# The last mixing of a four-block graph network: the weighed sum made on TensorE instead of VectorE

## The reference, cut to what matters

```
topk_vals, topk_idx = jax.lax.top_k(gate_logits, K)          # K = 2 of 16 experts
topk_w = jax.nn.softmax(topk_vals, axis=-1)
...
moe = jnp.sum(topk_w[..., None] * sel, axis=2)               # the two experts' outputs, weighed
y = x + moe
mu = jnp.mean(y, axis=-1, keepdims=True)
var = jnp.var(y, axis=-1, keepdims=True)
return (y - mu) / jnp.sqrt(var + EPS) * gamma + beta
...
x = x + _L1_ffn_ref(_layernorm(x, axis=-1)[None], ...)[0]
```

## Time and profile before

| what | value |
| --- | --- |
| median of 3 runs | 1766.2 us (1765.77 to 1766.2) |
| the profiled execution | 1768.76 us |
| its span (first to last instruction) | 1766.9 us |
| mean granted TensorE clock | 0.899 of full |
| PE busy | 1476.3 us (84%) |
| DVE busy | 869.2 us (49%) |
| ACT busy | 476.8 us (27%) |
| POOL busy | 337.7 us (19%) |

### The profile page before, as it was taken

One profiled execution on the slowest core, in us unless ns is written; L12 is line 12 of the kernel. 1 busy time (PEld: TensorE's weight loads), 2 busy tenths in 40 slices (PEclk: granted clock), 3 DMA queues, 4 the chain that ended last, 5 costly groups with the idle time before them and its releaser, 6 DMA issues. The chain is left out here.

```text
span 1766.9 us, 34489 instructions
## 1 busy us (share of the span) xinstructions
PE 1476.3 (84%) x8498; PEld 1032.0 (58%) x8499; DVE 869.2 (49%) x2496; ACT 476.8 (27%) x1228; POOL 337.7 (19%) x391
## 2 busy tenths in 40 slices
PE   4795999989998999957999947998997759999920
PEld 3674754457444845536998923445664648898810
DVE  6896743233232467773222257213887542222258
ACT  2464410012000311112444423001222314444421
POOL 3000210012000300013445510000000514545420
PEclk9955999999999999977999979998999569999965
DMA  4000321123111422221323267202221434333344
GB/s 122 0 0 11 99 84 47 50 84 119 48 47 54 128 90 86 84 95 65 113 92 126 80 184 217 71 24 81 72 71 30 156 125 128 121 100 97 124 129 128
DMA packets 134622, 158.41 MB, mean 90 GB/s; under 512 B 16929, under 2 KB 119698, under 8 KB 134258
## 3 DMA queue, kind: packets, MB, share of 16 engines
q1 hardware_dynamic: 122642, 125.59, 22.5%
q0 software_dynamic: 11840, 32.12, 6.1%
q10 hardware_dynamic: 96, 0.20, 0.0%
HBM read 103.12 MB, written 57.93 MB: 91 GB/s over the span
## 5 line engine op out<-in xcount | busy, mean ns | idle before, releaser
L885 PE MATMUL layer_ps<-parts,counts 128*128 128x512 f16 x1875 | 413.4, 382 | 1.3 <-issue 0.6
L885 PEld LDWEIGHTS layer_ps<-parts,counts 128*128 (+1 forms) x1875 | 184.5, 98 | 221.3 <-issue 8.7
L1526 ACT ACTIVATE experts_hT<-experts_ps_h,experts_b_col 128x128 f32<-128x128 f32 x456 | 166.2, 368 | 223.7 <-PE experts_ps_h L1501 142.4
L1509 PE MATMUL experts_ps_y<-experts_rows,experts_hT 128*128 128x256 f32 x688 | 165.0, 381 | 1.3 <-ACT experts_hT L1526 0.9
L1464 POOL DMA_INDIRECT chosen<-experts_y,experts_row x116 | 114.9, 991 | 140.2 <-issue 127.1
L1453 POOL DMA_INDIRECT experts_fetched<-tokens,experts_index x120 | 116.4, 970 | 105.6 <-issue 66.3
L1550 DVE COPY experts_xT<-experts_ps_x 128x256 f32<-128x256 f32 x114 | 48.4, 425 | 174.3 <-PE experts_ps_x L1490 157.6
L1509 PEld LDWEIGHTS experts_ps_y<-experts_rows,experts_hT 128*128 128x128 f32 x688 | 123.5, 191 | 17.4 <-ACT experts_hT L1526 3.7
L786 POOL TENSOR_TENSOR parts<-layer_rest,gru_rows 128x256 f32 (+2 forms) x75 | 54.6, 728 | 406.9 <-DVE layer_rest L761 406.9
L1501 PE MATMUL experts_ps_h<-experts_xT,experts_rows 128*128 128x128 f32 x976 | 122.1, 279 | 11.3 <-issue 10.2
L1501 PEld LDWEIGHTS experts_ps_h<-experts_xT,experts_rows 128*128 128x128 f32 x976 | 118.9, 194 | 19.9 <-issue 16.2
(11 more groups left out here) (310 smaller groups left out, 2072.8 us busy)
## 6 DMA issues: line engine op xcount, KB each, us to landing
experts_rows<-in_L_ffn_w SPq DMA_DIRECT2D x32, 512.0 KB
gru_rows<-x SPq DMA_DIRECT2D x75, 128.0 KB, 2.1
own<-layer_own SPq DMA_DIRECT2D x75, 128.0 KB, 1.7
layer_own_in<-own SPq DMA_DIRECT2D x75, 128.0 KB, 2.1
h<-layer_out SPq DMA_DIRECT2D x50, 128.0 KB, 1.7
gru_rows<-h SPq DMA_DIRECT2D x50, 128.0 KB, 2.1
gru_rows<-chosen SPq DMA_DIRECT2D x50, 128.0 KB, 2.4
combine_y<-chosen SPq DMA_DIRECT2D x50, 128.0 KB, 2.1
```

Source lines behind the costliest of these rows:

```text
L885: last = nc.tensor.matmul(ps[b][:], cst.counts[:, s, bass.ds(t * P, P)], parts[:, s, :], start=s == 0, stop=s == NT - 1)
L1509: last = nc.tensor.matmul(ps_y[:, 0:D], hT[:, c, :], down[b][:, c, :], start=c == 0, stop=c == KH - 1)
L1526: nc.scalar.activation(hT[:, c, :], ps_h[c][:, 0:P], function, bias=b1_col[:, bass.ds(e * KH + c, 1)]).then_inc(hT_ready, 1)
```

## The change

TensorE now makes the weighed sum. ScalarE writes, for each tile, two 128x128 matrices that hold a tile's weights on the diagonal (the identity times a weight a row). TensorE multiplies them with y0 and y1 and the identity with `tokens`, and sums all three in one of four product banks (PSUM). VectorE reads the statistics and the centring from the bank. SyncE's store of a tile is issued one step later, behind the load that follows.

```diff
-        mixed, out, small = pair("mixed", [P, D]), pair("out", [P, D]), pair("small", [P, 10])
-        normal, scale, w_loaded = pair("normal", [P, D]), sb("gamma", [P, D]), sem("w_loaded")
+        weigh = [pair(f"weigh{c}_", [P, P]) for c in range(2)]
+        out, small, normal = pair("out", [P, D]), pair("small", [P, 10]), pair("normal", [P, D])
+        scale, w_loaded = sb("gamma", [P, D]), sem("w_loaded")
+        ps = [ctx.enter_context(nc.psum_tensor(tag + f"ps{b}", [P, BANK], F32)) for b in range(B)]
...
-        loop = lambda engine, step: tile_loop(engine, step, n=B, ahead=2, behind=2)
+        loop = lambda engine, step: tile_loop(engine, step, n=B, ahead=2, behind=B)
...
                 def step(k, b):
                     t = k * B + b
-                    sp.wait_ge(taken, t + 1)
+                    sp.wait_ge(mixed, t + 1)
                     if not past(t + B):
                         load(t + B, b)
-                    sp.wait_ge(ready, t + 1)
-                    if past(t + 1):
...
+                    if not early(t - 1):
+                        store(t - 1, b - 1)
...
+            @block.tensor
+            def _(pe):
+                def step(k, b):
+                    t = k * B + b
+                    pe.wait_ge(got[b], k * 32 + 32)
+                    pe.wait_ge(weights_ready, t + 1)
+                    if not early(t - B):
+                        pe.wait_ge(centred, t - (B - 1))
+                    for c in range(2):
+                        nc.tensor.matmul(ps[b][:, 0:D], weigh[c][b % 2][:], y[b][c][:], start=c == 0, stop=False)
+                    nc.tensor.matmul(ps[b][:, 0:D], cst.ident[:], tile_of(tokens, t), start=False, stop=True).then_inc(mixed, 1)
+
+                loop(pe, step)
 
             @block.scalar
             def _(act):
                 nc.scalar.preload_act_table(ACT.Sqrt)
 
+                def spread_weights(t, b):
+                    if not early(t - 2):
+                        act.wait_ge(mixed, t - 1)
+                    nc.scalar.activation(weigh[0][b][:], cst.ident[:], ACT.Copy, scale=plan.weight[0][:, bass.ds(t, 1)])
+                    nc.scalar.activation(weigh[1][b][:], cst.ident[:], ACT.Copy,
+                                         scale=plan.weight[1][:, bass.ds(t, 1)]).then_inc(weights_ready, 1)
+
                 def step(k, b):
-                    act.wait_ge(var_ready, k * B + b + 1)
+                    t = k * B + b
+                    if not past(t + 2):
+                        spread_weights(t + 2, b % 2)
+                    act.wait_ge(var_ready, t + 1)
                     norm_root(nc, cst, small[b % 2]).then_inc(std_ready, 1)
 
+                for t in range(2):
+                    spread_weights(t, t)
                 loop(act, step)
...
                 def norm_of(u, b):
-                    nc.vector.scalar_tensor_tensor(normal[b][:], mixed[b][:], small[b][:, 6:7], scale[:], ALU.subtract,
+                    nc.vector.scalar_tensor_tensor(normal[b % 2][:], ps[b][:, 0:D], small[b % 2][:, 6:7], scale[:], ALU.subtract,
                                                    ALU.mult).then_inc(centred, 1)
...
-                    dve.wait_ge(got[b], k * 32 + 32)
-                    nc.vector.scalar_tensor_tensor(mixed[d][:], y[b][0][:], plan.weight[0][:, bass.ds(t, 1)],
-                                                   tile_of(tokens, t), ALU.mult, ALU.add).then_inc(begun, 1)
+                    dve.wait_ge(mixed, t + 1)
+                    nc.vector.bn_stats(small[d][:, 0:6], ps[b][:, 0:D])
                     if behind:
                         if early(t - 2):
                             dve.wait_ge(w_loaded, 16)
                         inverse_of(t - 1, before_d)
-                        norm_of(t - 1, before_d)
-                    dve.wait_ge(begun, t + 1)
-                    nc.vector.scalar_tensor_tensor(mixed[d][:], y[b][1][:], plan.weight[1][:, bass.ds(t, 1)], mixed[d][:],
-                                                   ALU.mult, ALU.add).then_inc(taken, 1)
+                        norm_of(t - 1, (b - 1) % B)
+                    dve.drain()
+                    nc.vector.bn_aggr(small[d][:, 6:8], small[d][:, 0:6]).then_inc(var_ready, 1)
                     if behind:
-                        dve.wait_ge(inverted, t)
-                        dve.wait_ge(centred, t)
                         last_of(t - 1, before_use, before_d)
-                    dve.wait_ge(taken, t + 1)
-                    nc.vector.bn_stats(small[d][:, 0:6], mixed[d][:])
-                    dve.drain()
-                    nc.vector.bn_aggr(small[d][:, 6:8], small[d][:, 0:6]).then_inc(var_ready, 1)
...
                 inverse_of(u, d)
-                dve.drain()
-                norm_of(u, d)
-                dve.drain()
+                norm_of(u, (NT - 1) % B)
                 last_of(u, use, d)
```

More of the change, by code:

```diff
@@ L1803, in combine @@
         y = [[sb(f"y{b}_{c}", [P, D]) for c in range(2)] for b in range(B)]
-        mixed, out, small = pair("mixed", [P, D]), pair("out", [P, D]), pair("small", [P, 10])
-        normal, scale, w_loaded = pair("normal", [P, D]), sb("gamma", [P, D]), sem("w_loaded")
+        weigh = [pair(f"weigh{c}_", [P, P]) for c in range(2)]
+        out, small, normal = pair("out", [P, D]), pair("small", [P, 10]), pair("normal", [P, D])
+        scale, w_loaded = sb("gamma", [P, D]), sem("w_loaded")
+        ps = [ctx.enter_context(nc.psum_tensor(tag + f"ps{b}", [P, BANK], F32)) for b in range(B)]
         got = [sem(f"got{b}") for b in range(B)]
         stored = [sem(f"stored{b}") for b in range(2)]
-        var_ready, std_ready, taken = sem("var_ready"), sem("std_ready"), sem("taken")
-        begun, inverted, centred, ready = sem("begun"), sem("inverted"), sem("centred"), sem("ready")
-        loop = lambda engine, step: tile_loop(engine, step, n=B, ahead=2, behind=2)
+        weights_ready, mixed, var_ready, std_ready = sem("weights_ready"), sem("mixed"), sem("var_ready"), sem("std_ready")
+        inverted, centred, ready = sem("inverted"), sem("centred"), sem("ready")
+        loop = lambda engine, step: tile_loop(engine, step, n=B, ahead=2, behind=B)
         buffer = lambda k, b: (k * 2 + b // 2, b % 2)
@@ L1822, in step, with store @@
                     t = k * B + b
-                    sp.wait_ge(taken, t + 1)
+                    sp.wait_ge(mixed, t + 1)
                     if not past(t + B):
                         load(t + B, b)
-                    sp.wait_ge(ready, t + 1)
-                    if past(t + 1):
-                        sp.dma_start(output[t * P:N_NODES, :], out[b % 2][0:LAST, :]).then_inc(stored[b % 2], 16)
+                    if not early(t - 1):
+                        store(t - 1, b - 1)
+                def store(u, b):
+                    sp.wait_ge(ready, u + 1)
+                    if past(u + 1):
+                        sp.dma_start(output[u * P:N_NODES, :], out[b % 2][0:LAST, :]).then_inc(stored[b % 2], 16)
                     else:
-                        sp.dma_start(output[rows(t), :], out[b % 2][:]).then_inc(stored[b % 2], 16)
+                        sp.dma_start(output[rows(u), :], out[b % 2][:]).then_inc(stored[b % 2], 16)
                 for b in range(B):
@@ L1836, in _ @@
                 tile_loop(sp, step, n=B, ahead=B, behind=2)
+                store(NT - 1, NT - 1)
                 for b in range(2):
                     sp.wait_ge(stored[b], 16 * uses(b))
+            @block.tensor
[10 more added lines that the diff above has]
+                loop(pe, step)
             @block.scalar
@@ L1851, in _, with inverse_of, last_of @@
             def _(dve):
+                def inverse_of(u, d):
+                    dve.wait_ge(std_ready, u + 1)
+                    nc.vector.reciprocal(small[d][:, 9:10], small[d][:, 8:9]).then_inc(inverted, 1)
                 def norm_of(u, b):
-                    nc.vector.scalar_tensor_tensor(normal[b][:], mixed[b][:], small[b][:, 6:7], scale[:], ALU.subtract,
+                    nc.vector.scalar_tensor_tensor(normal[b % 2][:], ps[b][:, 0:D], small[b % 2][:, 6:7], scale[:], ALU.subtract,
                                                    ALU.mult).then_inc(centred, 1)
[L1856 to L1860, removed]
+                def last_of(u, use, d):
+                    dve.wait_ge(centred, u + 1)
+                    dve.wait_ge(inverted, u + 1)
                     if not early(u - 2):
-                        dve.wait_ge(stored[b], use * 16)
-                    nc.vector.scalar_tensor_tensor(out[b][:], normal[b][:], small[b][:, 9:10], tile_of(base, u), ALU.mult,
+                        dve.wait_ge(stored[d], use * 16)
+                    nc.vector.scalar_tensor_tensor(out[d][:], normal[d][:], small[d][:, 9:10], tile_of(base, u), ALU.mult,
                                                    ALU.add).then_inc(ready, 1)
@@ L1870, in step @@
                     t = k * B + b
-                    use, d = buffer(k, b)
```

(19 more changed lines are left out.)

## The result

The changed kernel took 1751.81 us (median of 4 runs, 1750.59 to 1754.42) against 1765.99 us for the kernel before (median of 4, 1763.86 to 1766.2): 14.2 us less, a ratio of 0.9925 with a 95% interval of 0.9913 to 0.9937. Measured beside it two more times, on two different chips, the ratio was 0.9915 (0.9898 to 0.9931) and 0.9923 (0.9903 to 0.9943). The forecast was 1752.7 us, 13.5 less than a median of 1766.2.

What follows compares the result with a forecast made beforehand. VectorE's operations, a plain sum, bound the last stage; the start, loop tiles at 1.78 us, written-out tiles at 1.58 and the tail end it at 1748.2 against 1761.7, 13.5 less: 1752.7 us, 8-in-10 range 1748 to 1760.

Steps and rivals of the forecast that it cites:

- Two operations off VectorE's sum: Last stage: the two weighing operations leave VectorE (0.79 to 0.80 us a tile); its remaining five steps sum to 1.68.
- The loop's edge: Loop of the last stage, once in four tiles: taken as 2.353 - 2.32 us a tile, bringing VectorE's step to 1.71.
- A bank as source: VectorE reading a product bank instead of SBUF: extra cost put at 0, bounds -0.05 to +0.06 us a read.
- The loop's tile of 1.78: Forecast time per loop tile in us, from VectorE's 1.71 and SyncE's about 1.75 with hitches; bounds 1.60 and 2.0.
- SyncE's queue: Loop of the last stage: SyncE's three DMAs a tile were to take about 1.75 us, level with VectorE's 1.71.
- third rival: Loop step of 2.1 us instead of 1.78, by register work behind the drain or by transfers: 5.1 us more, 1757.8; chance 0.10.
- ScalarE's copies: Two 128x128 weight copies a tile on ScalarE: at most 0.84 us, some 1.4 with root and register work, hidden below 1.78.
- The start: Head of the last stage: bank 0 done 2.77 us after 1700.7, bank 1 at 1706.05, TensorE's clock rising after 5 us.
- The last four tiles: Written-out tiles at the stage's end, waits being constants: 1.58 us each, statistics of tile 20 at 1739.35, tile 24 at 1745.65.
- The tail behind the last statistics: End of VectorE's work: 0.93 us to the aggregation, 0.55 to the reciprocal, then 0.07, 0.52 and 0.48.
- TensorE as the bound: Rival: TensorE stays at 1.2 GHz, 2.56 us a tile in the last stage, 5.8 us slower, 1772; chance 0.07.

Runs made afterwards that it cites:

- four_one: Changed kernel with four output buffers instead of two and one 256 KB load a tile instead of two of 128: 1744.19 us, ratio 0.9903 to the kernel before.
- order_only: Kernel before with only the new order of operations and the later store, VectorE still making the weighed sum: 1766.92 us against 1765.55 before.
- one_load: Changed kernel with one 256 KB load a tile in place of two of 128 KB, same bytes: 1748.72 us, ratio 0.9918 to the kernel before.
- one_y: Changed kernel with the second expert's load left out, 256 KB of traffic a tile instead of 384: 1744.40 us, ratio 0.9902 to the kernel before.
- warm: Changed kernel with five extra 128x128 identity matmuls on TensorE at the head of the stage: 1748.56 us, ratio 0.9920 to the kernel before.

## Why the prediction was right

- **Two operations off VectorE's sum.** Right. The steps I gave as 0.34, 0.07, 0.52, 0.35 and 0.40 are 0.34, 0.07, 0.55, 0.32 and 0.40 in the tile above; both sums are 1.68. Over a whole round of four tiles it is less: in four_one, where VectorE waits for no store, aggregation to last operation is 0.23, 0.34, 0.31 and 0.23, and the tile 1.65. With the order alone (order_only) nothing is gained.
- **The loop's edge.** Misread. I spread 0.03 us a tile over ten tiles, but only one edge lies in them:

```profile
1738.14 0.42 DVE L1890 BATCH_NORM_STATS2 combine_small<-combine_mixed 128x6 f32<-128x256 f32 x1
...
1739.18 0.48 DVE L1875 SCALAR_TENSOR_TENSOR combine_mixed<-combine_y,mix_weight,tokens 128x256 f32<-128x256 f32 x1 [0.37 <-issue]
...
1740.88 0.42 DVE L1890 BATCH_NORM_STATS2 combine_small<-combine_mixed 128x6 f32<-128x256 f32 x1
```

  In the kernel before it costs some 0.4 us once in four tiles (2.74 between these statistics, 2.32 in the tile of the earlier trace rows), which makes the loop's tile 2.41. In the changed kernel no such step stands out (1.59 to 1.71 in four_one). So of the 0.76 us between 2.41 and 1.65, 0.79 are the two operations and 0.09 the edge, less some 0.12, most of which lies open behind the drain.
- **A bank as source.** I put 0; it is 0.1 us in all.
- **The loop's tile of 1.78.** The size is right (1.79, 1.77, 1.70), half of the reason is not. I let SyncE's queue pace it, "level with DVE's". SyncE does issue as reckoned (0.27 from store to load, 0.86 for the loads), but with one DMA less (one_load) nothing moves. VectorE's own step is about 1.65 and not 1.71, and in the first profile waits for stores add 2.1 us over the 16 tiles, 0.13 each; that the two give 1.78 together is luck. They come from landings, late under 221 GB/s (one_y). The prediction had this in its third rival, at a price of 5.1 us and a chance of 0.10; the mechanism was there, its size was 2. And with four output buffers one DMA less (four_one) does move the stage a little.
- **ScalarE's copies.** 390 ns each, two a tile, hidden as said, to within about a microsecond of the stage.
- **The start.** Bank 0 after 2.8 us by my sum, 2.97 measured. The clock rose 3.1 us after the first matmul and not 5, which brought bank 1 forward by 1.1 us. In the second profile it rose after 6.1 us and bank 1 came 2.56 after bank 0, as forecast:

```profile
1697.89 2.08 PE L1856 MATMUL combine_ps<-combine_y,combine_weigh 128*128 128x256 f32 x4 [10.70 <-DMA combine_y<-chosen]
...
1703.42 0.43 DVE L1910 BATCH_NORM_STATS2 combine_small<-combine_ps 128x6 f32<-128x256 f32 x1 [1.87 <-PE combine_ps L1857]
```

- **The last four tiles** were the mis-sized term: 6.3 us by my 1.58 a tile, 7.8 measured (1733.32 to 1741.14), of which 1.7 are three waits for stores; in the two other profiles it is 6.6 and 7.7. The earlier clock and this one nearly cancel: 47.5 us forecast from y0's arrival to VectorE's end, 48.2 measured. The tail behind the last statistics was 2.55 by the sum and 2.57 measured. So the stage gave 12.8 us in that profile, 0.7 less than the 13.5 forecast, while the medians gave 14.2, 0.7 more. What lies between the two comes from outside the stage or from the kernel before having one profile; that the whole came out so near is in part luck.
- **TensorE as the bound.** It did not come true; the clock was at 1.00 from 1700 until the end of its work. The price of that rival was sound: at 2.59 a tile the kernel is slower than before.

## What to carry to other kernels

Where one engine's operations add up to the stage with no waits between them, moving two of them to an idle engine is worth their start-to-start distance (0.79 us a tile here) less what then lies open (some 0.1, the waits behind the drain). The new sum can be read off neighbouring stages that already have the same pairs of operations. Take the cost of a loop's edge from whole rounds of the loop, not from a stretch that runs beyond it. A shorter step raises the traffic per microsecond, so look again at every buffer count that was set for the slower step: here two output buffers, enough at 160 GB/s, made VectorE wait 2.0 to 3.8 us at 221 to 226, of which four buffers gave back 1.0 to 2.0. To learn whether the queue or the bytes are late, change one at a time: fewer DMAs with the same bytes, then fewer bytes with the same DMAs.

## What the runs showed of the hardware that I had not expected

- The rise of TensorE's clock from 1.2 to 2.4 GHz came 3.1 us after the first matmul of the stage in one execution and 6.1 us in another of the same program, both times within an unbroken stream of 128x256 matmuls; 2.5 us of 128x128 matmuls and a pause of 0.70 ahead of it did not bring the first tile to the high clock (warm).
- One load of 256 KB lands later after its issue than two of 128 (median 3.4 us against 2.3), and stores behind it as well (2.7 against 2.0), at the same 221 to 223 GB/s.
- Stores issued from ScalarE's queue beside SyncE's loads landed later (2.8 us) than behind them on SyncE's own (2.0 to 2.2 in three profiles).
- VectorE's statistics and centring take as long from a product bank as from SBUF (426 against 422 ns, 466 and 466).
